# One add and one store of every node block moved from the last layer's sums into the transformer stage of a graph network, and a changed order of fetches, scatters and landing signals

## The reference

```
x3 = layernorm(x2 + L2(x2, edges))            # attention, then x + relu(xn @ W1 + b1) @ W2 + b2
h_neigh = segment_sum(x3[src], dst)            # last layer, L3
deg = segment_sum(1, dst)
out = ((h_neigh + x3) / (deg + 1)) @ W.T + b
out = out * a + x3 * (1 - a)                   # a = sigmoid(alpha)
out = layernorm(out) * gamma + beta
result = layernorm(x3 + out)
```

## Time and profile before

| | |
|---|---|
| median of 3 runs | 6378.78 us (6372.11 to 6390.99) |
| profiled execution | 6394.93 us, its span 6393.1 us |
| PE busy | 3612.9 us, 57% of the span |
| DVE busy | 3730.9 us, 58% |
| ACT busy | 2485.0 us, 39% |
| POOL busy | 2857.4 us, 45% |
| HBM | 185 GB/s over the span |

### The profile page before, as it was taken

One profiled execution on the slowest core, in us unless ns is written; L12 is line 12 of the kernel. 1 busy time (PEld: TensorE's weight loads), 2 busy tenths in 40 slices (PEclk: granted clock), 3 DMA queues, 4 the chain that ended last, 5 costly groups with the idle time before them and its releaser, 6 DMA issues. The chain is left out here.

```text
span 6393.1 us, 71923 instructions
## 1 busy us (share of the span) xinstructions
PE 3612.9 (57%) x20295; PEld 2852.9 (45%) x20406; DVE 3730.9 (58%) x11266; ACT 2485.0 (39%) x5939; POOL 2857.4 (45%) x2733
## 2 busy tenths in 40 slices
PE   5677751447732366631455523445599993775543
PEld 1344431447731255520355522344477772665443
DVE  9665530349954466622455554556576772665998
ACT  0233320339830155521122212444366662222776
POOL 0455567104557533376555504667255554553000
PEclk9898875679965689855677766666799996888666
DMA  8454541659957777621344355667344542786664
GB/s 322 134 149 142 146 145 41 226 203 299 310 166 253 245 252 256 229 81 44 110 118 119 115 191 140 231 214 246 129 165 165 180 171 77 255 267 219 209 209 164
DMA packets 705159, 1172.85 MB, mean 183 GB/s; under 512 B 110930, under 2 KB 454021, under 8 KB 698514
## 3 DMA queue, kind: packets, MB, share of 16 engines
q1 hardware_dynamic: 593392, 958.95, 45.8%
q0 software_dynamic: 103200, 183.16, 9.6%
q10 hardware_dynamic: 8172, 26.13, 1.0%
HBM read 689.93 MB, written 490.39 MB: 185 GB/s over the span
## 5 line engine op out<-in xcount | busy, mean ns | idle before, releaser
L2148 POOL DMA_INDIRECT sc_rows<-layer,node_idx x400 | 378.5, 946 | 316.1 <-DVE sc_xin L2163 163.2
L1978 PE MATMUL ro_end<-vals,end_mask 128*2 128x128 f32 x1600 | 242.0, 316 | 384.2 <-DVE vals L1842 225.2
L1337 POOL DMA_INDIRECT cap_own<-layer,w_own x200 | 206.3, 1031 | 482.1 <-SPq L1317 429.4
L2627 POOL DMA_INDIRECT tf_edge_x<-x,tf_src_idx x200 | 192.1, 961 | 387.4 <-SPq L2610 337.4
L2751 PE MATMUL tf_h_ps<-tf_x_t,tf_w 128*128 128x512 f32 x784 | 351.4, 601 | 24.0 <-ACT tf_hidden L2712 22.9
L2763 PE MATMUL tf_o_ps<-tf_w,tf_hidden 128*128 128x128 f32 (+1 forms) x3136 | 361.8, 276 | 3.9 <-issue 3.7
L2763 PEld LDWEIGHTS tf_o_ps<-tf_w,tf_hidden 128*128 128x128 f32 (+1 forms) x3136 | 356.3, 192 | 5.7 <-issue 5.4
L1978 PEld LDWEIGHTS ro_end<-vals,end_mask 128*2 128x2 f32 x1600 | 147.7, 96 | 468.9 <-DVE vals L1842 233.2
L2004 PE MATMUL ro_acc<-vals,ro_mask 128*126 128x128 f32 x1600 | 242.9, 316 | 197.4 <-ACT ro_square L1936 134.0
L2712 ACT ACTIVATE tf_hidden<-tf_h_ps,tf_b 128x512 f32<-128x512 f32 x392 | 268.7, 687 | 216.2 <-PE tf_h_ps L2751 151.6
L722 POOL DMA_INDIRECT agg<-mean_sums,d_last x200 | 221.0, 1105 | 243.8 <-ACT mean_sums L767 195.7
(11 more groups left out here) (486 smaller groups left out, 11666.3 us busy)
## 6 DMA issues: line engine op xcount, KB each, us to landing
ro_mask<-masks SPq DMA_DIRECT2D x100, 504.0 KB
layer<-zeros SPq DMA_DIRECT2D x96, 512.0 KB
si_both<-layer SPq DMA_DIRECT2D x48, 1024.0 KB
ro_far<-far SPq DMA_DIRECT2D x75, 512.0 KB
ro_both<-both SPq DMA_DIRECT2D x75, 512.0 KB
agg<-zeros SPq DMA_DIRECT2D x48, 512.0 KB
x<-zeros SPq DMA_DIRECT2D x48, 512.0 KB
mom_x<-in_x_dram SPq DMA_DIRECT2D x48, 512.0 KB
```

What stands on the lines that cost most here:

```text
L1978: mm = nc.tensor.matmul(end_ps[0:2, j, :], k.end_mask[:, t, :], k.vals[:, t, :], start=True, stop=True, skip_group_check=True)
L2148: nc.gpsimd.indirect_dma_start(out=rows[:, g % SC, c * GT + j, :], out_offset=None, in_=k.layer1, in_offset=bass.IndirectOffsetOnAxis(ap=k ...
```

## The change

1. `shifted` = x3 + beta is no longer made in `OwnPart.mix_in` from a reloaded x3. The transformer makes it on VectorE from the x3 tile in SBUF (`shift`, lag 5, last in VectorE's list) and SP stores it (`store_shifted`, lag 6, last in SP's list). beta is loaded with the transformer's constants. ScalarE's `finish` also waits for the `shift` of two blocks before, which reads the same x3 buffer.
2. SP's `landed` goes from the end of its list to the front, ahead of the loads.
3. GpSimd's list goes from (fetch, lag 0), (send, lag 2) to (send, lag 1), (fetch, lag 0): each group's rows are scattered before the next group's are fetched.

```
-                pipeline(NG + 1, (load, 0), (store, 4), (landed, 5))
+                def store_shifted(n):
+                    sp.wait_ge(s["shifted"], n + 1)
+                    sp.dma_start(node_rows(k.shifted, n, tail(n)), shifted[0:tail(n), n % 2, :, :])\
+                      .then_inc(s[f"shift_put{n % 2}"], 16)
+
+                pipeline(NG + 1, (landed, 5), (load, 0), (store, 4), (store_shifted, 6))
+                sp.wait_ge(s["shift_put0"], 16 * (NG // 2 + 1))
+                sp.wait_ge(s["shift_put1"], 16 * (NG // 2))
...
-                pipeline(EG, (fetch, 0), (send, 2))
+                pipeline(EG, (send, 1), (fetch, 0))
...
+                def shift(n):
+                    u, p = n % 2, tail(n)
+                    dve.wait_ge(s["x3_made"], n + 1)
+                    if n >= 2:
+                        dve.wait_ge(s[f"shift_put{u}"], n // 2 * 16)
+                    v.tensor_tensor(shifted[0:p, u, :, :], x3[0:p, u, :, :],
+                                    beta[0:p, :].unsqueeze(1).broadcast_to([p, NJ, D]),
+                                    ALU.add).then_inc(s["shifted"], 1)
...
-                pipeline(NG + 1, (second, 1), (third, 3), (lambda n: norms[1].negate(dve, n, n % 2, tail(n)), 4), (first, 0))
+                pipeline(NG + 1, (second, 1), (third, 3), (lambda n: norms[1].negate(dve, n, n % 2, tail(n)), 4), (first, 0),
+                         (shift, 5))
...
                     if n >= 2:
                         act.wait_ge(s[f"stored{u}"], n // 2 * 16)
+                        act.wait_ge(s["shifted"], n - 1)
...
         if n >= 2:
             sp.wait_ge(s["weighed"], n - 1)
-            sp.wait_ge(s["shifted"], n - 1)
             sp.wait_ge(self.conv.turned, n - 1)
...
-        sp.wait_ge(s["shifted"], n + 1)
-        sp.dma_start(node_rows(self.k.shifted, n, tail(n)), self.shifted[0:tail(n), u, :, :])\
-          .then_inc(s[f"shift_put{u}"], 16)
         sp.wait_ge(s["own_made"], n + 1)
...
-        if n >= 2:
-            dve.wait_ge(s[f"shift_put{u}"], n // 2 * 16)
-        dve.tensor_tensor(self.shifted[0:p, u, :, :], self.x3[0:p, u, :, :], wide(self.beta),
-                          ALU.add).then_inc(s["shifted"], 1)
         dve.wait_ge(s["mixed"], n + 1)
```

More of the change, by code:

```diff
@@ L2556, in transformer_phase @@
         x_t = sb("x_t", [P, 2, NJ, P])
+        shifted = sb("shifted", [P, 2, NJ, D])
+        beta = sb("beta", [P, D])
         edge_x = sb("edge_x", [P, XS, GT, D])
@@ L2566, in transformer_phase @@
         names = (["xm_made", "rest_made", "normed", "turned", "x_copied", "hidden_made", "bent", "out_made", "x3_added",
-                  "x3_made", "stored0", "stored1", "w_step", "w_made", "last_in", "unit_step", "indexed", "landed"]
+                  "x3_made", "stored0", "stored1", "shifted", "shift_put0", "shift_put1", "w_step", "w_made", "last_in", "unit_step", "indexed", "landed"]
                  + [f"{x}_in{u}" for x in ("x2", "msum", "rest") for u in range(TL)])
@@ L2572, in transformer_phase @@
                            (g2[:, :], a["L2_gnn_g2"].rearrange("(p r) -> p r", r=1)),
-                           (be2[:, :], a["L2_gnn_be2"].rearrange("(p r) -> p r", r=1))]
+                           (be2[:, :], a["L2_gnn_be2"].rearrange("(p r) -> p r", r=1)),
+                           (beta[:, :], a["L3_gnn_beta"].partition_broadcast(P))]
                        + [(b1[:, b:b + 1], a["L2_gnn_b1"][b * P:(b + 1) * P].rearrange("(p r) -> p r", r=1))
@@ L2781, in sb @@
             return k.sb(st, "op_" + name, shape)
-        self.w, self.w_t, self.bias, self.beta = sb("w", [P, D]), sb("w_t", [P, D]), sb("bias", [P, D]), sb("beta", [P, D])
+        self.w, self.w_t, self.bias = sb("w", [P, D]), sb("w_t", [P, D]), sb("bias", [P, D])
         self.gamma, self.mix, self.floor = sb("gamma", [P, D]), sb("mix", [P, 4]), sb("floor", [P, NCOL])
-        self.x3, self.part, self.own, self.shifted = (sb(x, [P, 2, NJ, D]) for x in ("x3", "part", "own", "shifted"))
+        self.x3, self.part, self.own = (sb(x, [P, 2, NJ, D]) for x in ("x3", "part", "own"))
         load_constants(k, [(self.w[:, :], a["L3_gnn_W"]), (self.bias[:, :], a["L3_gnn_b"].partition_broadcast(P)),
                            (self.gamma[:, :], a["L3_gnn_gamma"].partition_broadcast(P)),
-                           (self.beta[:, :], a["L3_gnn_beta"].partition_broadcast(P)),
                            (self.mix[:, 0:1], a["L3_gnn_alpha"].partition_broadcast(P))])
@@ L2822, in begin @@
         self.conv = Linear(k, st, "op_conv", self.w_t[:, :])
-        names = ["ready0", "ready1", "mixed", "weighed", "shifted", "own_made", "own_put0", "own_put1", "shift_put0",
-                 "shift_put1"]
+        names = ["ready0", "ready1", "mixed", "weighed", "own_made", "own_put0", "own_put1"]
         self.s = {x: k.sem(st, "op_" + x) for x in names}
@@ L2852, in close_sync @@
     def close_sync(self, sp):
-        for what in ("own_put", "shift_put"):
-            sp.wait_ge(self.s[what + "0"], 16 * (NG // 2 + 1))
-            sp.wait_ge(self.s[what + "1"], 16 * (NG // 2))
+        sp.wait_ge(self.s["own_put0"], 16 * (NG // 2 + 1))
+        sp.wait_ge(self.s["own_put1"], 16 * (NG // 2))
     def open_vector(self, dve):
```

## The result

The changed kernel takes 6330.16 us in the median of 7 runs (6306.48 to 6352.12), the kernel before 6386.57 (6372.11 to 6401.05, 7 runs, taken together with it). The ratio is 0.9908, 95% interval 0.9889 to 0.9928: 56 us faster. The forecast was 6300 with a range of 6278 to 6348. The profiled execution took 6339.04 us, its span 6337.2.

The account below looks back on a forecast made before the run. TensorE was taken to pace the transformer, GpSimd's indirect DMAs its tail, and VectorE's wait for shifted's store the sums. Gains 70.6 + 2 + 6.4 = 79 us off the 6378.78 us median gave 6300, range 6278 to 6348.

Parts of the forecast that it names:

- Part 1: Sums of the last layer without shifted's add, wait and store: period 8.87 to 7.4 us, gain 70.6 us over 48.
- The floor of 7.17 us: Sums: shortest period of the TensorE and ScalarE loop, everything at the 2.4 GHz level and no load late.
- 7.4: Sums: period in us taken for the forecast, near the floor, between bounds of 7.17 and 8.87.
- Rival B: Sums: the wait was worth little, period 8.65 us, gain 19 us in all, 6360 us; chance 0.07.
- Rival A: Sums: late loads take the wait's place, period 8.1 us, gain 45 us in all, 6334 us; chance 0.22.
- The stage's end: End of the sums: own's last store no longer queues behind shifted's slow last tile; gain 0 to 8.3, taken 2 us.
- Part 2: Transformer: the added add and store, and loads waiting behind SP's landing wait, are hidden by slack; cost 0.
- C: Transformer: SP's landing wait starves xm, once store plus load landing exceed 14.8 us; slower, up to 6423 us; chance 0.05.
- shared port of SBUF: Transformer: the moved add could hold one GpSimd DMA per block up to 1.23 us; at most 5 us, taken 0.
- Part 3: GpSimd's order at the transformer's tail: last send at 5385.1, gain 6.4 us; bounds gain 10.8 and loss 4.8.
- four landings G: Transformer's tail: four sends each wait for their fetch to land, taken as 2 us each, bounds 0.9 and 4.8.
- The price at light load: Transformer's tail: with 0.2 us per memory access, G sits at its low end and part 3 gains about 10 us.

Follow-up runs that it names:

- e11: Changed kernel with the last block's loads and stores cut into 96 and 10 partitions, run again in the third group: 5653.05 us, ratio 0.9817.
- e12: Changed kernel with the last block cut and each fetch ahead of the previous group's send, run again: 5639.68 us, ratio 0.9791.
- e5: Kernel before with four buffers of shifted in place of two, add and store still in the sums: 6273.73 us, ratio 0.9912.
- e7: Changed kernel with every load and store of the last block, from the transformer on, cut into 96 and 10 partitions: 6210.66 us, ratio 0.9807.
- the first group: Four kernels on one chip: both kernels unedited, the new order alone, the moved add and store alone; kernel before there 5757.42 us.
- e9: Changed kernel storing shifted three times, two to unread tables, all ahead of the store of x3: 5701.08 us, ratio 0.9897.
- e10: Changed kernel storing shifted five times, all ahead of the store of x3: 5820.69 us, ratio 1.011 to the kernel before.
- e2_after: Changed kernel with no edit, run again on another chip (also written e2): 5688.96 us, ratio 0.9881 to the kernel before.
- e3: Kernel before with only the new place of landed and the new GpSimd order, shifted still in the sums: 5756.48 us, ratio 0.9998.
- e6: Changed kernel with the fetch of the next group ahead of the send of this one: 6271.47 us, ratio 0.9898.
- e4: Kernel before with only the add and store of shifted moved to the transformer, orders otherwise kept: 5691.8 us, ratio 0.9883.
- e1: Kernel before with no edit, run against itself: 5757.77 us, ratio 1.0004.
- e8: Changed kernel with the last block cut into 96 and 10 partitions and the next fetch ahead of the send: 6237.85 us, ratio 0.9849.

## Why the prediction was right, and where it was not

**Part 1, right in mechanism and size.** 70.6 us were forecast, 71.3 and 65.9 came. The floor of 7.17 us was exact (7.18 in the timeline; 344.5 us for 48 periods in e11 and e12). That 7.4 met the mean of 7.33 is in part luck: it stood for some products at the lower clock, but the granted clock between the first and the last op_own is 0.99 and 48 of the 49 products are short, and the 7.8 us above the floor come mostly from the last block, where row_b is late behind a tile of 434 KB. e5 shows that the removed wait, and not the removed work, is most of the gain. Rival B is refuted by that. Rival A has its waits (95.0 us at mean_same) but not its price: only at the last block does one of them reach TensorE.

**The stage's end.** 2 us taken, 2.0 and 3.0 measured. The bound of 8.3 does not stand: e7 took the slow store away and the stage's end kept 24.4 us, 9 of them with nothing on any engine or queue. From the issue of the last own to the next load 16.7 and 16.3 us became 14.3 and 13.3, and 12.8 is the least in any run.

**Part 2, right.** Cost 0 forecast, +1.8 us in the first group, -7.8 in the first pair of profiles, where the uneven blocks of the slower chip blur it. The load of x2 is issued 2.75 us behind the store of x3 (3.45 were reckoned), the loads land in 6.2 us (6.1), and xm starts 9.35 us behind the store (10.45). e9 and e10 bracket the point from which C decides.

On the shared port of SBUF: in e2_after 85 of GpSimd's DMAs in the transformer run beside one of the moved adds, and they take 969 ns in the median, the other 274 take 970. The longer one that the Trainium skill, SBUF — State Buffer, section "SBUF: two separate sides", would have allowed for the moved add, if the issue of a DMA counts as a GpSimd operation that reads SBUF, does not show.

**Part 3, the term that was mis-sized: four landings G at 2 us.** "A send now waits for its own fetch to land" holds. In the profile after, the part's 32 DMAs take 41.3 us for the 40.6 reckoned, but the four landings take 1.9, 4.9, 3.8 and 3.9, 14.5 us for 8. Two of them fall behind the last tiles of x3 and shifted, which crawl on two DMA engines (cut, in e7, the two are 2.3 and 2.5 us; without shifted there, in e3, they are 5.1 and 2.5). The prediction had set shifted's last tile aside as "over by 5373"; its last packet ends at 5388.9. The fourth is 3.9 us in e7 and e11 too and 4.4 in e3, so no slow tile makes it. The tail gained 2.8 and 2.6 us where 6.4 were forecast for the part. The 6.4 already held 4.1 us by which the last blocks would be late; with the transformer's +1.8 counted in, the first group shows a gain of 0.8. e3 has a tail 5.6 us shorter; e6, with no landing waited for, one of 48.7 us for 55.2. On the totals of e2 and e4 the part cannot be told from nothing.

The price at light load that the prediction worked out, a gain of about 10 us, is not borne out: none of these four landings is under 1.8 us in any run. The Trainium skill, DMA: Bandwidth & Descriptors, section "Latency and other measured facts", calls its 0.2 us the average of a memory access, and not that at light load; the same row gives a DMA a fixed cost of about 2 us, which is near the first of the four, 1.9, and not near the others.

**The sum.** From the first xm on, 79 us were forecast and 83.3 and 65.4 measured in profiles; of the second, 3.8 us are missing in part 3, 4.7 in the sums (there the kernel before had been faster, 8.71 us a period for 8.82), and 4.1 on the way to the first op_own. That 83.3 lies so near 79 is in part luck: without the transformer's -7.8 it would be 75.5. The median of 6330 is 30 above the forecast: 8 because the kernel before stands at 6387 and no longer at 6379, and 22 that the 27.4 us ahead of the transformer account for (less the 4 us gained beyond 79). The change leaves the code there as it was. Among the twelve other profiles the same stretch scatters by 13 us within the first and third groups (3935.7 to 3949.2) and by 15 within the second, with no order by kernel. Whether 27 us is such a scatter, large, or an effect of where code and tensors lie, stays open: none of the groups had the kernel before at 6387 us, and no experiment tried it there. Against chance in one execution speaks that a gain of 83 us would be a ratio of 0.987, outside the measured 0.9889 to 0.9928.

## What to carry to other kernels

A store that a small ring of buffers makes the producer wait for can cost more than the work beside it: first give it buffers, or move it to a stage where that engine waits anyway, and sum the next loop from one period's timeline, which was good to 0.2% here. Before changing the order of issues at a stage's end, look at the last, odd-sized tile: its loads and stores may set the end of every stage that touches it, and cutting it gave here about half of what the whole change gave (34 us between the medians of e6 and e8 on one chip, 37 by the ratios of e11 and e2).

## What the runs showed of the hardware that was not expected

- A tile of 106 partitions moves at 52 GB/s with two of sixteen DMA engines busy (share 0.13); cut into 96 and 10, the three loads of the last block are there 7.0 us behind the first issue and not after 22.0. The Trainium skill, DMA: Bandwidth & Descriptors, section "Why a DMA increments its semaphore by 16 and not by 1", says that the number of engines is the largest up to 16 that divides the slowest dimension of both sides, and names 16 for 96 partitions; worked out from that rule, it is 2 for 106 and 10 for 10. For 106 the trace agrees; for the two pieces the runs show only that they are fast.
- At the transformer's end a send waits about 1.9 us for its gather where little else moves, 3.8 and 4.9 beside such a crawling tile, and 3.9 for the last one with nothing else moving, whose packets take 384 ns for the 119 of the gather before. The DMA engines are busy only 0.23 in the tail as a whole.
- The chips differ, and nearly all of it is ahead of the transformer (4555.7 us of the profile of before, 3937.7 of e1's): the kernel before takes 6387 and 6331 us on two and 5757 and 5761 on the two others, while the sums of the changed kernel take 352.0 us on the first and 352.0 in the first group, to the tenth.
- In the transformer, engines stand still with "remote" as the only releaser, up to 17 us on VectorE and 21 on ScalarE (e8). All six profiles of the two slower chips have it, none of the eight of the two faster ones, the same kernels among them. Its cause is open.
